# Second cross attention of a perceiver layer stack: scores from stored fp16 parts of the context

## What is computed

```python
x = x + L0_xattn(layernorm(x), ctx)      # 16 heads of 64, keys and values from ctx
x = x + L0_attn(layernorm(x))            # causal, 128 x 128
x = x + L0_ffn(layernorm(x))             # ternary weights
x = x + L1_xattn(layernorm(x), ctx)      # one head of 256
x = x + L1_attn(layernorm(x))            # selective scan
x = x + L1_ffn(layernorm(x))             # 8 experts, top 2, and a shared one

def L1_xattn(x, ctx):
    Q, K, V = x @ Wq + bq, ctx @ Wk + bk, ctx @ Wv + bv
    scores = clip(Q @ K.T / sqrt(256), -100, 100)
    return softmax(scores) @ V
```

## Time and profile before

| | |
|---|---|
| median of 3 runs | 1222.01 us (1221.83 to 1223.29) |
| profiled execution | 1227.61 us, its span 1225.9 us |
| TensorE busy | 1157.2 us (94%) |
| VectorE busy | 905.3 us (74%) |
| ScalarE busy | 898.8 us (73%) |
| GpSimd busy | 587.1 us (48%) |
| mean granted clock of TensorE | 0.983 of full speed |
| scores of the second attention | 955.97 to about 1002.6 us |

### The profile page before, as it was taken

The page is one execution under the profiler, slowest core; times in us unless marked ns, Lnnn a source line. Parts: engine busy times, 40 slices in busy tenths (PEclk is TensorE's granted clock), DMA queues, the critical chain, the costliest instruction groups (busy, mean ns, idle before and its releaser), DMA issues. The chain is left out here.

```text
span 1225.9 us, 31791 instructions
## 1 busy us (share of the span) xinstructions
PE 1157.2 (94%) x12394; PEld 800.2 (65%) x12395; DVE 905.3 (74%) x1721; ACT 898.8 (73%) x1548; POOL 587.1 (48%) x548
## 2 busy tenths in 40 slices
PE   4899999999999999999999999999977979889898
PEld 2466666666666666666666666666656448744698
DVE  7677878887888888888787878787744569679632
ACT  4599988888888888888888888888841539386010
POOL 6165656565656565656565656565540420133000
PEclk8999999999999999999999999999989999989999
DMA  6364634444444444444444444444427674040274
GB/s 213 76 178 105 157 88 121 96 116 94 108 105 109 105 111 102 107 107 94 120 108 107 109 105 109 103 91 96 92 76 239 242 268 151 1 173 0 82 285 178
DMA packets 139186, 151.06 MB, mean 123 GB/s; under 512 B 17904, under 2 KB 126736, under 8 KB 139040
## 3 DMA queue, kind: packets, MB, share of 16 engines
q1 hardware_dynamic: 138496, 146.97, 44.5%
q10 hardware_dynamic: 544, 2.10, 0.5%
HBM read 72.25 MB, written 0.15 MB: 59 GB/s over the span
## 5 line engine op out<-in xcount | busy, mean ns | idle before, releaser
L456 POOL TENSOR_TENSOR pT_lo<-p_exp,pT_hi 128x896 f16<-128x896 f32 x223 | 420.6, 1886 | 323.8 <-ACT pT_hi L555 323.8
L536 ACT ACTIVATE p_exp<-ps,ln_k,esc 128x896 f32<-128x896 f32 x224 | 245.7, 1097 | 55.3 <-PE ps L897 47.4
L669 DVE TENSOR_REDUCE tile_max<-ps 128x128 f16<-128x896 f32 x224 | 244.4, 1091 | 49.9 <-PE ps L873 47.2
L555 ACT ACTIVATE pT_hi<-p_exp 128x896 f16<-128x896 f32 x224 | 211.7, 945 | 0.9
L664 DVE TENSOR_TENSOR v_lo<-ps,v_hi 128x512 f16<-128x512 f32 x196 | 135.5, 692 | 74.7 <-ACT v_hi L528 72.3
L860 PE MATMUL ps<-c_hi,wk_hi 128*128 128x448 f16 x448 | 159.3, 356 | 6.2 <-DVE c_lo L651 4.7
L915 PE MATMUL ps<-v_lo,pT_hi 128*128 128x64 f16 x1568 | 164.4, 193 | 0.0
L914 PE MATMUL ps<-v_hi,pT_hi 128*128 128x65 f16 x1568 | 164.3, 193 | 0.1
L916 PE MATMUL ps<-v_hi,pT_lo 128*128 128x65 f16 x1568 | 163.8, 193 | 0.0
L860 PE MATMUL ps<-c_hi,wk_lo 128*128 128x448 f16 x448 | 158.8, 354 | 0.0
L860 PE MATMUL ps<-c_lo,wk_hi 128*128 128x448 f16 x448 | 158.8, 354 | 0.0
(11 more groups left out here) (350 smaller groups left out, 2074.8 us busy)
## 6 DMA issues: line engine op xcount, KB each, us to landing
k_st<-k_top SPq DMA_DIRECT2D x444, 112.0 KB, 2.3
k_st<-k_rest SPq DMA_DIRECT2D x444, 56.0 KB, 2.0
c_raw<-in_ctxT SPq DMA_DIRECT2D x14, 896.0 KB, 5.5
xa_ct<-in_ctxT SPq DMA_DIRECT2D x14, 896.0 KB, 6.3
xa_cn<-in_ctx SPq DMA_DIRECT2D x14, 896.0 KB, 7.5
me_w<-in_me_w SPq DMA_DIRECT2D x8, 1536.0 KB, 6.2
me_w<-in_me_w SPq DMA_DIRECT2D x8, 768.0 KB, 5.7
ss_c_all<-ss_bc SPq DMA_DIRECT2D x4, 512.0 KB, 5.9
```

Of the source, the lines that this page charges most:

```text
L456: nc.gpsimd.tensor_tensor(pT_lo[:, n % 2, :, :].rearrange("p t s -> p (t s)"), p_exp[:, n % 2, :], pT_hi[:, n % 2, :, :].rearrange("p t s ...
L536: nc.scalar.activation(p_exp[:, n % 2, :], s_scores[n % 2], ACT.Exp, bias=ln_k[:, 0:1], scale=esc[:, n // H0 % 2:n // H0 % 2 + 1]).then_in ...
L555: nc.scalar.activation(pT_hi[:, n % 2, :, :].rearrange("p t s -> p (t s)"), p_exp[:, n % 2, :], ACT.Copy).then_inc(pT_hi_ready, 1)
L669: nc.vector.tensor_reduce(tile_max[:, n % 2, :], s_scores[n % 2].rearrange("p (t s) -> p s t", s=S), AX.X, ALU.max).then_inc(tile_max_done, 1)
```

## The change

The scores of the second attention are made from the fp16 parts that the first attention has computed anyway.

- In the first attention, SyncE stores both parts of every chunk to a tensor in memory, `parts`: 28 transfers of 448 KB, those of chunk c + 1 at steps h = 10 and 12 of chunk c, those of chunk 0 at n = 13 and 14. Before ScalarE overwrites a `c_hi` buffer it also waits for the stores of two chunks before (`parts_saved`). `un` keeps all chunks' units, and `w_inv` stays allocated.
- The ring `xa.ct` holds both parts in fp16, as many bytes as one fp32 chunk, and is loaded from `parts`. Three more chunks (3, 4 and 5) are loaded during the ternary feed-forward, behind the scan's weights, into the part of `sc` that the clips of chunks 8 to 13 write later. In the second attention SyncE therefore loads chunks 6 to 13. Context rows come behind chunks 7, 8, 8, 10 and 12.
- The query is multiplied by `w_inv`, its largest absolute value is found and spread over the partitions by a product with ones, and it is scaled and split into `q2_hi` (ScalarE) and `q2_lo` (VectorE). Scores are then three fp16 products, 12 matmuls a chunk.
- Scores come out in units of a chunk: the factor `f` of each chunk is applied as the scale of the exponential, the clip uses bounds divided by it (`lims`), and the maxima are multiplied by it before the overall maximum.
- The last chunk's clip is done after the overall maximum; the last exponential and the second group of transposes wait for it, and the PSUM places of the transposes are exchanged.

```diff
+        un = sb("un", [P, NCH + 1])
+        w_inv = sb("w_inv", [P, DC])
+        parts = nc.dram_tensor("ctx_parts", [NCH, P, 2, DC, CH], F16).ap()
+        parts_saved = sem("parts_saved")
...
+                def save_part(c, low):
+                    sp.wait_ge(c_lo_ready, 4 * (c + 1))
+                    sp.dma_start(parts[c, :, low, :, :], (c_hi, c_lo)[low][:, c % 2, :, :]).then_inc(parts_saved, 16)
...
+                    if n == 13 or n == 14:
+                        save_part(0, n - 13)
+                    if h in (10, 12) and c + 1 < NCH:
+                        save_part(c + 1, (h - 10) // 2)
...
+                        act.wait_ge(parts_saved, 32 * (c - 1))
...
-                    nc.vector.tensor_scalar(un[:, par:par + 1], s_bound(c), 1.0 / C_TOP, un[:, 1 - par:2 - par], ALU.mult, ALU.max).then_inc(un_ready, 1)
+                    nc.vector.tensor_scalar(un[:, c + 1:c + 2], s_bound(c), 1.0 / C_TOP, un[:, c:c + 1], ALU.mult, ALU.max).then_inc(un_ready, 1)
...
+MORE = 3
+SPARE = 8
+Q2_TOP = 32768.0
-ROWS_BEHIND = (4, 7, 9, 11, 13)
+ROWS_BEHIND = (7, 8, 8, 10, 12)
...
-    xa.ct = sb("xa_ct", [P, RING, DC, CH], F32, scope)
+    xa.ct = sb("xa_ct", [P, RING, 2, DC, CH], F16, scope)
+    xa.sc = sb("xa_sc", [P, SK], F32, scope)
+    spare = [xa.sc[:, (SPARE + 2 * k) * CH:(SPARE + 2 * k + 2) * CH].bitcast(F16).rearrange("p (t c n) -> p t c n", t=2, c=DC) for k in range(MORE)]
...
-    def load_ct(sp, c, slot):
-        sp.dma_start(xa.ct[:, slot, :, :], ctxT[:, :, bass.ds(c * CH, CH)]).then_inc(xa.ct_loaded[slot], 16)
+    def ct_place(c):
+        return spare[c - RING] if RING <= c < RING + MORE else xa.ct[:, c % RING, :, :, :]
+
+    def ct_wait(engine, c):
+        if RING <= c < RING + MORE:
+            engine.wait_ge(xa.more_loaded, 16 * MORE)
+        else:
+            engine.wait_ge(xa.ct_loaded[c % RING], 16 if c < RING else 16 * (c // RING))
+
+    def load_ct(sp, c):
+        sp.wait_ge(parts_saved, 32 * NCH)
+        sp.dma_start(ct_place(c), parts[c]).then_inc(xa.more_loaded if RING <= c < RING + MORE else xa.ct_loaded[c % RING], 16)
...
                 ss.load(sp)
+                for c in range(RING, RING + MORE):
+                    xa.load_ct(sp, c)
...
-        t_ps = [[ps[:, 4, :], ps[:, 5, :]], [ps[:, 2, :], ps[:, 3, :]]]
-        low_marks = []
+        t_ps = [[ps[:, 2, :], ps[:, 3, :]], [ps[:, 4, :], ps[:, 5, :]]]
...
+                link(nc.gpsimd.memset(ones[:, :], 1.0))
+                marks["ones"] = link.count
...
-                for c in range(RING, NCH):
-                    sp.wait_ge(E["scores_done"], c - (RING - 1))
-                    xa.load_ct(sp, c, c % RING)
-                    if c in ROWS_BEHIND:
-                        context_rows(RING + ROWS_BEHIND.index(c))
-                for c in range(RING + len(ROWS_BEHIND), NCH):
+                row = RING
+                for c in range(RING + MORE, NCH):
+                    sp.wait_ge(E["scores_done"], c - RING - MORE + 1 if c < 2 * RING + MORE else c - RING + 1)
+                    xa.load_ct(sp, c)
+                    for _ in range(ROWS_BEHIND.count(c)):
+                        context_rows(row)
+                        row += 1
+                for c in range(row, NCH):
...
-                act.wait_ge(E["q2_done"], 1)
-                nc.scalar.activation(q2T[:, :, :], ps[:, 2, 0:DC * S].rearrange("p (c s) -> p c s", c=DC), ACT.Copy).then_inc(E["q2_ready"], 1)
+                act.wait_ge(E["q2_ready"], 1)
+                nc.scalar.activation(q2_hi[:, :, :], q2s[:, :, :], ACT.Copy, scale=q_scale[:, 0:1]).then_inc(E["q2_ready"], 1)
...
+                    if c == NCH - 1:
+                        act.wait_ge(E["clipped"], 2 * NCH)
+                    nc.scalar.activation(p[:, c % 2, :], sc[:, c * CH:(c + 1) * CH], ACT.Exp, bias=neg_top[:, 0:1], scale=f[:, c:c + 1],
...
+                link(nc.vector.tensor_tensor(q2s[:, :, :], ps[:, 2, 0:DC * S].rearrange("p (c s) -> p c s", c=DC),
+                                             w_inv[:, :].unsqueeze(2).to_broadcast([P, DC, S]), ALU.mult))
+                link(nc.vector.tensor_reduce(q_peak[:, :], q2s[:, :, :], AX.XY, ALU.max, apply_absolute_value=True))
+                marks["q_peak"] = link.count
                 link(nc.vector.tensor_scalar(lim[:, 0:1], ps[:, 6, 0:1], -1.0, -100.0, ALU.mult, ALU.add))
                 link(nc.vector.tensor_scalar(lim[:, 1:2], ps[:, 6, 0:1], -1.0, 100.0, ALU.mult, ALU.add))
-
-                for c in range(NCH):
+                v.wait_ge(E["q2_done"], 2)
+                link(nc.vector.tensor_scalar(q_un[:, :], ps[:, 0, 0:1], 1.0 / Q2_TOP, TINY, ALU.mult, ALU.max))
+                nc.vector.reciprocal(q_scale[:, :], q_un[:, :]).then_inc(E["q2_ready"], 1)
+                v.wait_ge(E["q2_ready"], 2)
+                nc.vector.scalar_tensor_tensor(out=q2_lo[:, :, :], in0=q2s[:, :, :], scalar=q_scale[:, 0:1], in1=q2_hi[:, :, :],
+                                               op0=ALU.mult, op1=ALU.subtract).then_inc(E["q2_ready"], 1)
+                link(nc.vector.tensor_scalar(f[:, :], un[:, 1:NCH + 1], q_un[:, 0:1], 1.0 / W_TOP, ALU.mult, ALU.mult))
+                link(nc.vector.reciprocal(f_inv[:, :], f[:, :]))
+                for k in range(2):
+                    link(nc.vector.tensor_scalar(lims[:, k, :], f_inv[:, :], lim[:, k:k + 1], None, ALU.mult))
+
+                def measure(c):
                     v.wait_ge(E["scores_done"], c + 1)
                     nc.vector.tensor_reduce(chunk_max[:, c:c + 1], sc_ps[c % 2], AX.XY, ALU.max).then_inc(E["clipped"], 1)
+
+                def clip(c):
                     nc.vector.tensor_scalar(sc[:, c * CH:(c + 1) * CH].rearrange("p (b k) -> p b k", b=2), sc_ps[c % 2],
-                                            lim[:, 0:1], lim[:, 1:2], ALU.max, ALU.min).then_inc(E["clipped"], 1)
-                v.wait_ge(E["clipped"], 2 * NCH)
+                                            lims[:, 0, c:c + 1], lims[:, 1, c:c + 1], ALU.max, ALU.min).then_inc(E["clipped"], 1)
+
+                for c in range(NCH - 1):
+                    measure(c)
+                    clip(c)
+                measure(NCH - 1)
+                v.wait_ge(E["clipped"], 2 * NCH - 1)
+                link(nc.vector.tensor_tensor(chunk_max[:, :], chunk_max[:, :], f[:, :], ALU.mult))
                 link(nc.vector.tensor_reduce(top[:, :], chunk_max[:, :], AX.X, ALU.max))
                 link(nc.vector.tensor_scalar(top[:, :], top[:, :], lim[:, 0:1], lim[:, 1:2], ALU.max, ALU.min))
                 nc.vector.tensor_scalar(neg_top[:, :], top[:, :], -1.0, LN_K, ALU.mult, ALU.add).then_inc(E["top_ready"], 1)
+                clip(NCH - 1)
...
-                pe.wait_ge(E["q2_ready"], 1)
+                pe.wait_ge(plink.sem, marks["ones"])
+                pe.wait_ge(vlink.sem, marks["q_peak"])
+                nc.tensor.matmul(ps[:, 0, 0:1], ones[:, :], q_peak[:, :], start=True, stop=True).then_inc(E["q2_done"], 1)
+                pe.wait_ge(E["q2_ready"], 3)
 
                 for c in range(NCH):
-                    slot = c % RING
-                    pe.wait_ge(ct_loaded[slot], c // RING * 16 + 16)
+                    ct = xa.ct_place(c)
+                    xa.ct_wait(pe, c)
                     at_least(pe, E["clipped"], 2 * (c - 1))
                     for k in range(DC):
-                        for b in range(2):
-                            mm = nc.tensor.matmul(sc_ps[c % 2][:, b, :], q2T[:, k, :], ct[:, slot, k, b * HCH:(b + 1) * HCH],
-                                                  start=(k == 0), stop=(k == DC - 1))
+                        for q2, low in ((q2_hi, 0), (q2_hi, 1), (q2_lo, 0)):
+                            for b in range(2):
+                                mm = nc.tensor.matmul(sc_ps[c % 2][:, b, :], q2[:, k, :], ct[:, low, k, b * HCH:(b + 1) * HCH],
+                                                      start=(k == 0 and low == 0 and q2 is q2_hi), stop=(k == DC - 1 and q2 is q2_lo))
                     mm.then_inc(E["scores_done"], 1)
-                pe.wait_ge(E["clipped"], 2 * NCH)
+                pe.wait_ge(E["clipped"], 2 * NCH - 2)
 
                 def turn_p(c):
                     pe.wait_ge(E["p_ready"], c + 1)
+                    if c == 1:
+                        pe.wait_ge(E["clipped"], 2 * NCH)
```

More of the change, by code:

```diff
@@ L136, in perceiver @@
         base = (x, z, y, zT, ident, st, stats, rows, cols, ps)
-        first_cross_attention(nc, ctx, a, sb, sem, *base[:9], gate, ps, *links, shared, loaded, ca_w, tf_wq, tf_mean, nat)
+        first_cross_attention(nc, ctx, a, sb, sem, *base[:9], gate, ps, *links, shared, loaded, ca_w, tf_wq, tf_mean, nat, un, w_inv, parts, parts_saved)
         with ExitStack() as late:
@@ L141, in perceiver @@
             with ExitStack() as mid:
-                xa = context_stream(a, mid, sb, sem)
+                xa = context_stream(a, mid, sb, sem, parts, parts_saved)
```

(32 more changed lines are left out.)

12 lines of the change are left out of this document (6 added, 6 removed).

## The result

The changed kernel takes 1220.16 us (median of 20 runs, 1217.80 to 1225.54); the kernel before, run beside it, 1223.47 us (median of 20, 1221.83 to 1228.94). The ratio is 0.9976, with a 95% interval of 0.9966 to 0.9986: 2.9 us faster (1.7 to 4.2), just outside what a measurement of this kernel can tell from nothing. The forecast was 5.65 us. The time is inside the range, the direction is right, and half of the gain is missing.

What follows compares the result with a forecast made beforehand. Second-attention scores were taken as led by TensorE with loads right behind. Stage -5.35, clip -1.0, exponential +0.2, stores +0.5 sum to -5.65 us, from the 1222.01 median to 1216.4; range 1211.5 to 1222.

Steps and rivals of the forecast that it cites:

- The bound: Second attention's scores: TensorE leads with loads right behind; 13 loads of 2.38 us, not 15, before the last score.
- the matmuls: Second attention's scores: 12 fp16 matmuls a chunk, 2.24 us in place of 3.0; without loads 2.45 us a chunk.
- The failed term: Second attention's scores: last chunk measured at 997.2 us in place of 1002.55, -5.35 us, the query's 2.2 included.
- the split: Start of the second attention: scaling and splitting the query delays the scores to about 958.2 us, +2.2 us.
- the first load: Second attention: chunk 0, done at 960.75 us, issues chunk 6's load; bytes flow from 962.15.
- The list of loads: Second attention: 8 chunk and 5 row loads in SyncE's order at 2.38 us each; chunk 13 landed at 994.2.
- the signs: Changed profile: first exponential about 5.9 us sooner, TensorE chunk waits 6 to 8 us; wrong if the stage's clock drops.
- The clock rival: Second attention: TensorE's clock falls in pauses, +2.2 us at the start, +2.2 at the last chunk; 1218.6 to 1220.9, chance 0.10.
- The clip: Last maximum to first exponential: a small product (0.2) takes the place of the last clip's 1.2 us step, -1.0 us.
- The exponential: Second attention's 14 exponentials: a scale per partition costs 0 to 1.1 us in all, taken as +0.2.
- The stores: First attention: 28 stores of the parts may delay key copies, nothing to 10.3 us, taken as +0.5; slower rival's chance 0.13.
- The early loads: Before the second attention: three chunks' loads hide behind the block's end; at most 2 us late if SyncE's slack were gone.

Runs made afterwards that it cites:

- e7_both: The change plus identity products around the query's split, five chunks loaded ahead, context rows 6 and 7 behind the last chunk; 1212.68 us, ratio to before 0.9909.
- e1_stores: The kernel before plus the 28 stores of the parts and ScalarE's wait for them, nothing read back; 1225.71 us against 1225.23, ratio 1.0002.
- e3_ahead: The kernel before, still fp32 without split or stores, with chunks 3 to 5 loaded early and the change's row order; ratio to before 0.9980.

## Why the prediction was wrong, and what in it was right

**The bound and the matmuls: right.** Loads stand behind the last scores (half the bytes shorten the stage by 4.7 us), and without them the round is 2.41 us a chunk against 2.45 in the sum. Four fp16 matmuls take 0.92 us where the clock is full.

**The failed term: -5.35 us for the stage, by its first two lines, the split and the first load.** The text had scores at 958.2 (+9.95) and chunk 0 measured at +12.5. They came at +11.0 and +15.8. Of the 3.3 us, the chain's start is 0.5 late (the multiply from PSUM at 950.50, +7.8; with identity products in the fastest kernel +7.3), the chain itself 0.5 longer (3.17 us for 2.66; among others 0.51 and 0.48 for the two casts put at 0.40, and a product of 0.56 put at 0.30), and 2.2 are chunk 0's twelve matmuls at 1.2 GHz (4.77 us from first matmul to maximum, against 2.55). The list of loads is played from the first issue, so all of them are 3.3 us late (chunk 11 was to be issued at +32.15 and was at +35.31), and the DMA engines idle meanwhile. The last chunk was to be measured at +48.95 and was at +53.65: 4.7 us late, of which 3.3 is this; the remaining 1.4 is the ring around chunk 11, issued at 977.99 behind chunk 10 and rows 6 and landed at 986.7, 8.7 us later where the text had 7.0. The 3.61 us that TensorE stood for it go before a second low clock, in which it worked until 990; by the last chunk that cost nothing, since TensorE waited again, 0.71 us, for chunk 13. The text took the pauses of 1.06 and 1.59 us as harmless since waits of 1.2 us had passed without a fall. But those stood among full work, these around one tiny product; and in this profile the clock had fallen before them, at 949.2, and did not rise in them. With the identity products the change is 7.8 us faster than before (0.9936; 5.4 to 10.2 by its interval), and 5.65 were forecast: the low clock is enough to account for the missing half.

Of the signs that the text gave, two spoke: the clock fell within the stage, and the first exponential came 1.6 us sooner and not 5.9. TensorE waited 4.8 us for chunks, at chunks 9, 11 and 13, where 6 to 8 at chunk 10 and later were forecast.

**The clock rival** had the place and the price at the start right (2.2 us), and too small a chance, 0.10. Its second 2.2 us, at the last chunk, the profile doesn't show. Its own sum gave 1218.6 to 1220.9; that the median, 1220.16, lies in it is in part luck, since the late 1.4 us above have another cause. What the text had not seen is that the trace of before, with a clock of 1.00 throughout, was itself one of several cases: of the three profiles with fp32 scores two have a fall in the block's first 10 us. The Trainium skill (TensorE: Matmul & The Clock Gate, HAM oscillation) describes compute shorter than the waits for its loads; the trace has that at chunk 11, but at the start no load is waited for, only a chain of VectorE and ScalarE.

**The clip: right**, -1.0 forecast, -0.9 in the profile (2.03 for 2.94), -1.1 in the pair. **The exponential**: 0.09 us each, inside its bounds, the sum's +0.2 neither confirmed nor refuted. **The stores**: put at +0.5, measured at 0.2 with an interval of -1.3 to 1.8. **The early loads** are hidden behind the block's end, as forecast: the stretch from the first attention's end, 910.65, to 942.68 is 32.0 us, before it was 33.1. Since the clock was low for 7.8 us of the one and 9.6 of the other, e7_both is the better pair: 33.1 us with 9.6 us low, the same as before.

**What the sum of the profile gives.** Stage -0.65, clip -0.9: -1.6 us by the first exponential, against -2.9 in the timed runs. Profiles differ here by run: with stores alone, where this stage is untouched, the first exponential came at +58.1 and not +57.2, and against that the change gains 2.4. The stretch from the first exponential to the next block took 139.7 to 139.8 us in five of the profiles with fp16 scores, 141.0 to 141.3 in the four others, and 141.5 to 142.4 in the three with fp32 scores. It goes with the time at the lower clock there, by windows of 1 us: 10.2 us in each of the five, 13.6 to 13.7 in the four and in e1_stores (141.5), 17.0 to 17.1 in the kernel before and e3_ahead (both 142.4). At like clock the fp16 and the fp32 kernels are within 0.2 to 0.5 us, so the change gains little or nothing of its own there. Whether it also shifts the odds of the clock's falls stays open; no run was aimed at it.

## What to carry to other kernels

A short chain of small operations in front of a stage costs more than its own length if the stage's first result also issues the stage's first load: then every load shifts, and an engine that stood idle in the chain may do the first chunk at half clock. When a stage is bound by loads, look at what stands in the queue in front of its last ones before making its arithmetic cheaper: moving two row loads from there took 4.7 us off the stage in the profiles, while the new arithmetic, with all it needed, did no better than loading three chunks ahead alone. Loading further ahead with the rows left in place gained nothing that the runs show. And one profile with a clock of 1.00 does not say that the stretch is safe: the same code had the fall at other places, or not at all.

## What the runs showed of the hardware

- Eight 128-column identity matmuls that nothing reads made the kernel 4.9 and 4.4 us faster in two pairs; with them the first score did not run at the low clock in any of five profiles.
- At the block's start the granted clock fell at one of a few places of the same code, or not at all. Over the change's timed runs the time goes with its mean: the seven at 0.980 and below have a median of 1222.5 us, the nine at 0.982 and above 1219.55.
- Chunk 11, issued with chunk 10 and one row load outstanding in front of it (and the end of chunk 9), took 8.7 us to land, at 395 GB/s for the core as a whole, while the first two of the stage took 5.2 and 4.6, and chunks 9 and 10 took 5.2 and 4.9.
